# Window attention on one Trainium2 core: the order of exponentials, copies and a bias product inside a software pipeline

## The reference

```
xn = layernorm(h)
q, k, v = split(xn @ qkv_weight.T + qkv_bias)        # 64 windows, 8 heads, 128 x 8
attn = softmax(q * 8**-0.5 @ k.T + relative_bias)    # 64 x 8 matrices of 128 x 128
h = h + (attn @ v) @ proj_weight.T + proj_bias
```

## Time and profile before

| | us |
|---|---|
| median of 3 runs | 1490.92 (1488.49 to 1492.17) |
| the profiled execution's own time | 1492.72 |
| its span in the trace | 1490.8 |
| PE busy in the span | 1335.4 (90%) |
| DVE, ACT, POOL busy | 887.4, 860.3, 613.7 |

### The profile page before, as it was taken

One profiled execution on the slowest core, in us unless ns is written; L12 is line 12 of the kernel. 1 busy time (PEld: TensorE's weight loads), 2 busy tenths in 40 slices (PEclk: granted clock), 3 DMA queues, 4 the chain that ended last, 5 costly groups with the idle time before them and its releaser, 6 DMA issues.

```text
span 1490.8 us, 43422 instructions
## 1 busy us (share of the span) xinstructions
PE 1335.4 (90%) x15780; PEld 880.4 (59%) x15780; DVE 887.4 (60%) x2815; ACT 860.3 (58%) x2649; POOL 613.7 (41%) x967
## 2 busy tenths in 40 slices
PE   6998997888888888799999998799999999969998
PEld 2446874444444444577777777456666666446665
DVE  3775774555555555577878886234555555655664
ACT  3975663777777777455555555235555555635553
POOL 5000113555655655435555564412333333225554
PEclk9997996999999999899999999659999999969999
DMA  8300000000000000000000000000000000000001
GB/s 222 70 1 0 1 1 1 2 0 0 0 0 0 0 0 0 2 3 0 0 0 0 0 0 1 1 0 2 0 0 0 0 0 1 0 0 10 15 14 23
DMA packets 10094, 13.79 MB, mean 9 GB/s; under 512 B 9136, under 2 KB 9136, under 8 KB 9520
## 3 DMA queue, kind: packets, MB, share of 16 engines
q1 hardware_dynamic: 10032, 12.95, 3.5%
HBM read 10.85 MB, written 2.10 MB: 9 GB/s over the span
## 4 chain that ended last, share of the span: by engine, by line
PE 72%; ACT 10%; DVE 9%; issue 6%; POOL 1%; DMA 1%; ACTq 0%; DVEq 0%; POOLq 0%; SPq 0%
PE bank L1318 6%; PE bank L588 5%; PE bank L591 5%; PE bank L632 5%; PE bank L1655 4%; PE bank L145 4%; PE bank L1673 4%; PE bank L1312 4%; ACT big L689 3%; PE bank L1007 2%; PE bank L1277 2%; PE bank L1342 2%; ACT big L696 2%; PE bank L1034 2%; PE bank L324 2%
## 5 line engine op out<-in xcount | busy, mean ns | idle before, releaser
L527 POOL TENSOR_TENSOR big<-big 128x512 f32<-128x512 f32 x128 | 133.0, 1039 | 153.7 <-DVE big L725 153.6
L632 PE MATMUL bank<-cst,big 128*128 128x128 f32 x512 | 80.1, 279 | 53.5 <-ACT big L696 53.0
L632 PEld LDWEIGHTS bank<-cst,big 128*128 128x128 f32 x512 | 59.7, 142 | 104.5 <-issue 86.4
L1390 POOL TENSOR_TENSOR big<-g_a,g_b 64x64 f32 x128 | 40.0, 312 | 191.1 <-DVE g_a L1380 191.1
L929 POOL TENSOR_TENSOR big<-big 128x512 f32<-128x512 f32 x64 | 65.6, 1045 | 113.8 <-DVE big L1183 113.8
L689 ACT ACTIVATE big<-big 128x128 f32<-128x128 f32 x256 | 100.0, 405 | 1.2 <-DVE big L737 1.2
L1709 ACT ACTIVATE big<-bank 128x512 f32<-128x512 f32 x128 | 66.2, 603 | 50.4 <-PE bank L1655 50.4
L1576 POOL TENSOR_TENSOR big<-big 128x512 f32<-128x512 f32 x48 | 60.9, 1270 | 74.8 <-DVE big L1779 72.2
L1357 ACT ACTIVATE g_r<-bank,g_bias 128x64 f32<-128x64 f32 x128 | 40.2, 314 | 88.6 <-PE bank L1318 88.5
L689 ACT ACTIVATE big<-bank,big 128x128 f32<-128x128 f32 x256 | 90.5, 370 | 0.0
L1342 PE MATMUL bank<-cst 128*128 128x256 f32 (+1 forms) x256 | 88.3, 426 | 0.0
(11 more groups left out here) (271 smaller groups left out, 3661.1 us busy)
## 6 DMA issues: line engine op xcount, KB each, us to landing
big<-x_dram SPq DMA_DIRECT2D x12, 512.0 KB, 8.0
cst<-consts_dram SPq DMA_DIRECT2D x1, 3364.5 KB, 22.4
out_dram<-h SPq DMA_DIRECT2D x8, 256.0 KB, 2.6
cst<-consts_dram SPq DMA_DIRECT2D x3, 256.0 KB
cst<-consts_dram SPq DMA_DIRECT2D x1, 279.5 KB, 3.0
a_proj_padded<-consts_dram SPq DMA_DIRECT2D x8, 2.0 KB
cst<-consts_dram SPq DMA_DIRECT2D x8, 2.0 KB
cst<-consts_dram SPq DMA_DIRECT2D x2, 4.0 KB
```

Of the source, the lines that this page charges most:

```text
L527: nc.gpsimd.tensor_tensor(P, P, a_rs[t % 4].unsqueeze(2).to_broadcast([128, 4, 128]), ALU.mult).then_inc(a_n_r, 1)
L632: m = nc.tensor.transpose(bank(4)[:, 128 * k:128 * (k + 1)], a_P[tb % 4][:, 128 * k:128 * (k + 1)], eye)
```

## The change

Three reorderings, with no instruction added or removed. In PE, the bias product of an odd item t+1 leaves the odd slot t-1 (behind the scores) for the even slot t, behind the transposes and (if u is not 0) the attended product, and ahead of rows and projection. In ACT, the rows copy and the queries go behind the exponentials and the copy out of bank 4. In DVE, the copy out of bank 4 goes ahead of the keys and the addition to h.

```diff
@@ stage2_pe
             m = nc.tensor.matmul(scores_bank(t), a_q[l][r, :], a_kz[l][r, :], start=True, stop=not t % 2)
-            if t % 2:
-                m = nc.tensor.matmul(scores_bank(t), eye, c("a_bias", 512, 1024), start=False, stop=True)
-            m.then_inc(a_sc_r, 1)
+            if t % 2 == 0:
+                m.then_inc(a_sc_r, 1)
+
+        def bias(t):
+            nc.tensor.matmul(scores_bank(t), eye, c("a_bias", 512, 1024), start=False, stop=True).then_inc(a_sc_r, 1)
...
                 for d in (1, 2):
                     if exists(i, (t + d) // 8):
                         scores(i + (t + d) // 8, (t + d) % 8)
+            if t % 2 == 0 and exists(i, 0):
+                bias(t + 1)
             if u == 0:
@@ stage2_act
-            if u == 0 and exists(i, l, N2 - 1):
-                rows(i + l, 1 - l)
             ib, tb = back(i, t, 1)
...
                 m.then_inc(a_e_r, 1)
-            if u == 1 and exists(i, l, N2 - 1):
-                queries(i + l, 1 - l)
             ib, tb = back(i, t, 3)
             if tb % 2 and exists(ib, 0):
                 act.wait_ge(a_pt_r, ib * 8 + (tb + 1))
                 nc.scalar.copy(a_PT[tb % 4], bank(4)).then_inc(a_pta_r, 1)
+            if u == 0 and exists(i, l, N2 - 1):
+                rows(i + l, 1 - l)
+            if u == 1 and exists(i, l, N2 - 1):
+                queries(i + l, 1 - l)
@@ stage2_dve
+            ib, tb = back(i, t, 3)
+            if tb % 2 == 0 and exists(ib, 0):
+                v.wait_ge(a_pt_r, ib * 8 + (tb + 1))
+                if tb >= 4 or exists(ib, -1):
+                    v.wait_ge(a_av_r, ib * 8 + (tb - 3))
+                nc.vector.tensor_copy(a_PT[tb % 4], bank(4)).then_inc(a_ptd_r, 1)
             if u == 1 and exists(i, l, N2 - 1):
                 keys(i + l, 1 - l)
...
-            ib, tb = back(i, t, 3)
-            if tb % 2 == 0 and exists(ib, 0):
-                ...
-                nc.vector.tensor_copy(a_PT[tb % 4], bank(4)).then_inc(a_ptd_r, 1)
```

More of the change, by code:

```diff
@@ L746, in slot @@
                 nc.vector.tensor_tensor(hp, hp, bank(3)[:, 128:256].rearrange("p (b c) -> p b c", c=C), ALU.add).then_inc(a_h_r, 1)
-            ib, tb = back(i, t, 3)
-            if tb % 2 == 0 and exists(ib, 0):
-                v.wait_ge(a_pt_r, ib * 8 + (tb + 1))
-                if tb >= 4 or exists(ib, -1):
-                    v.wait_ge(a_av_r, ib * 8 + (tb - 3))
-                nc.vector.tensor_copy(a_PT[tb % 4], bank(4)).then_inc(a_ptd_r, 1)
             if isinstance(i, int) and i == N2 and t in (2, 4):
```

## The result

The changed kernel takes 1449.96 us (median of 4 runs, 1446.92 to 1451.30) against 1491.47 for the kernel before beside it: a ratio of 0.9727, 95% interval 0.9706 to 0.9748. Forecast were 1450 and a range of 1431 to 1468. Its profiled execution took 1446.92, with a span of 1445.0. The kernel was run again later, with 0.9701 (0.9682 to 0.9720).

A forecast was written before the change was run, and what follows sets the result against it. The prediction took a PE-ACT-PE loop, set by ACT's instruction order, as the bound. Halves fall from 11.21 to 9.9 us: 38 us, plus 3 in the first slots, makes 41, so 1450 us, range 1431 to 1468.

The forecast's parts named there:

- The loop through ACT's order: Stage 2, u = 0: ACT's copy out of bank 4 queued behind the rows copy; reordering regains 1.44 us per half.
- T0 - 0.5 to T0 + 0.8: When ACT was to start the exponentials after the change; T0 is the start of PE's transposes at u = 0.
- The bias product moved: PE's 0.96 us product goes to the even slot, moved but not saved; the 0.48 us wait at u = 3 goes.
- The wait on the spread: PE's scores at u = 3 wait for POOL's spread of the keys: new wait of 0.56 to 0.70 us per half.
- The sum: A half (four slots) takes 9.9 us, gaining 1.3; 29 halves give 38 us, first slots 3, total 41.
- The first slots: Start of the stage: a 1.98 us wait before the transposes goes, 2 us, plus 1 us from less idling.
- The drain stays as it is: The stage's end: no gain, since there are no rows to copy.
- The rule weighed: DVE's L251 with two SBUF inputs over a POOL product: no cost by the trace, about 6 us by the skill's rule.
- A: Rival: the spread's wait is hidden, a half takes 9.3 to 9.6 us, total 1433; chance 0.13.
- B: Rival: ACT is part of the loop again, a half takes 10.6 us, total 1471; chance 0.20.
- C: Rival: slower, PE waits at qkv for ACT's late rows copy; a half of 11.9 us gives 1511; chance 0.05.
- D: Rival: no change, something beside ACT's order such as POOL's queue sets the pace, 1491; chance 0.04.

The follow-up runs named there:

- experiment 1: The kernel before with only the ACT reordering (exponentials and copy out of bank 4 ahead of rows copy and queries): 1444.42 us, ratio 0.9710.
- experiment 5: The full change, but ACT's rows copy stands ahead of the exponentials again, queries still behind: 1493.95 us, ratio 1.0011 to the kernel before.
- experiment 4: The full change without DVE's part (its copy out of bank 4 behind the keys again): 1449.92 us, ratio 0.9729 to the kernel before.
- experiment 7: The full change, with POOL's spread waiting for a count four lower, the scores that last read its keys: 1428.22 us, ratio 0.9597 to the kernel before.
- act_relaxed: The kernel before with only ACT's reordering and the spread's wait count lowered by four: 1442.97 us, ratio 0.9681.
- two_inputs: The kernel before plus one DVE addition of two SBUF constants in slots with u = 3, beside POOL's products: 1488.34 us in one run.
- dve_only: The kernel before with only DVE's copy out of bank 4 moved ahead of keys and the addition to h: 1487.17 us, ratio 0.9989.
- experiment 9: The run two_inputs: the kernel before plus a DVE addition with two SBUF inputs beside POOL's products, 1488.34 us.

## Why the prediction was right

**The loop through ACT's order.** Right, and shown from both sides: ScalarE's part alone gives the gain (experiment 1), and putting one copy back takes it away (experiment 5). The prediction gave the whole 1.44 us at u = 1 to it; in the trace after, the transposes at u = 1 follow the attended product after 0.36 us, without a wait:
```profile
509.43 0.43 PE L607 MATMUL bank<-big 128*32 128x128 f32 x8
509.79 0.66 PE L634 MATMUL bank<-cst,big 128*128 128x128 f32 x4
```
ACT was even earlier than laid out: its exponentials started 0.94 us ahead of the transposes at u = 0 (516.31 against 517.25), where the text had T0 - 0.5 to T0 + 0.8:
```profile
516.31 0.38 ACT L691 ACTIVATE big<-bank,big 128x128 f32<-128x128 f32 x1
```
So the cover by the bias product in the slot with u = 0 was never needed, as experiment 1 shows without it.

**The bias product moved.** The prediction had 0.48 us back at u = 3 and 0.6 lost on the spread. By these two terms the move loses 0.12 us. Measured are 9.81 us for a half with the product left where it was (experiment 1) and 9.99 with it moved (experiment 4): a loss of 0.18 us, of which VectorE's part gives 0.06 back (9.93). The prediction did not draw the conclusion that this move was worth nothing, though its own terms said so, and it gave VectorE's part no term of its own.

**The wait on the spread.** Foreseen at 0.56 to 0.70 us, taken as 0.6. The idle rows of PE give 0.50, and 0.1 more goes in the longer pair of scores (1.23 in place of 1.13). Experiment 7 takes exactly this wait away and gets 0.66 us of each half back. That it came from the place of the bias product follows from `act_relaxed`: with the product in its old place the looser count changes nothing in a half.

**The sum.** 9.9 us for a half was forecast and 9.93 measured; 29 x 1.3 = 38 against 36.0 in 28 halves and some 1.3 in the last. The first slots gave 5.0 in place of 3, as the clock no longer fell to 1.2 GHz there (granted 1.00 from 250 to 260 us after, 0.50 from 255 to 260 before); the text had 0 to 3 us for that and took 1, and it was the upper end. The drain gave 2 us in place of 0. "The drain stays as it is" was wrong for its slots: the wait of 0.4 us at u = 3 stood there too (595.06 to 595.90 before) and is gone, and PE needs 0.6 us less up to its first product of stage 3 with fX (L999 at 601.02, L1003 at 558.15). The other 1.3 us lie behind that product, where PE runs with long waits. Busy time from it to the mark behind the drain, before and after (columns as in the earlier trace rows):
```profile
601.02:618.57 17.55, 11.34 (x74) 7.89 (x71) 9.85 (x14) 3.40 (x7) 6.58 (x10) 0.65 0.00 1
558.15:574.37 16.22, 9.54 (x73) 5.99 (x70) 9.85 (x14) 3.53 (x7) 6.79 (x11) 0.79 0.00 1
```
DVE does the same work, PE takes 1.8 us more for its own at a granted clock of 0.65 against 0.79. Why the clock was lower there is not shown; the traces of `two_inputs` and `dve_only`, with PE's and ACT's order of before, had 38.5 and 38.4 us from the last L566 on in place of 39.2.

So the sum was right where the change acts, and that the median came out at 1449.96 for a forecast of 1450 is in part luck. Between the two traces lie 45.8 us and not 41: 2 more in the first slots, 2 in the drain, 1.6 behind it, 0.7 less in the halves. The 41.5 us between the two medians are less, because the profiled execution of before was 1.3 us above the median of its kernel, and that of the change 3.0 below. One bound of the forecast's own range was also summed wrongly: a wait of 0.3 us and 5 us in the first slots give 1450 - 29 x 0.3 - 2 = 1439, not 1442. The range of 1431 to 1468 does not hang on it.

**The rule weighed.** It had been given 6 us if L251 came to lie over a GpSimd product. It did not: L251 stayed at 424 to 426 ns, and L527 at 1035 to 1042, as DVE's reciprocal, for which GpSimd waits, comes right behind L251. In both traces each of the 14 L251 ends 0.2 us before the next L527 starts (before: 282.33 + 0.42 against 282.92). The rule itself holds (experiment 9). What the rows of before showed was that the two never met, not that meeting is free: the sentence "by the row the overlap costs nothing" was wrong.

**The rivals.** A (spread hidden, 1433) would have been seen as halves under 9.6; B and C as waits of L632 on L696 or of L572 on the rows copy. None of them is in the trace. D would have left the halves at 11.2.

## What to carry to other kernels

When one engine idles before an instruction that needs the newest result, and work that needs only old results stands behind it in the same queue, swap the two; here a copy of 0.27 us in the wrong place cost 3% of the program. Look up what a moved instruction counts for: the bias product raised a semaphore on which a third engine waited, four items stricter than needed, and that wait, not the product's own 0.96 us, decided whether the move paid. Test the parts of a reordering one by one: two of three here were worth nothing by themselves, and the bias move paid only after a wait outside the change was loosened. Whether VectorE's part is needed then was not run. And where the whole time moves by 2 us and more between traces for other reasons, judge such a change by the stretch in which it acts.

## What the runs showed that I had not expected

The chain of waits is of no help once a software pipeline is full: in the trace after, between 500 and 512 us, it leads through GpSimd and "issue", although PE was 95% busy from 400 to 500, and 100% with the spread's wait loosened (experiment 7), so that nothing else of GpSimd held it up. Its head in that window (pieces that reach over the edge count whole, so the shares add up to more than 100%):
```profile
by line: issue 65.9%; POOL big L527 35.2%; POOL rstd L269 5.8%; POOL h L509 3.4%; POOL big L513 3.0%; POOL eps_var L267 1.8%; POOLq L525 1.2%; POOL big L521 1.1%; POOLq L513 0.5%; POOLq L512 0.3%; POOLq L266 0.3%; POOLq L268 0.3%; POOLq L26
```
There the distances between the starts of one line, once per half, told more: in the three kernels that ran twice a half came out the same to 0.01 us (9.93, 9.81, 9.27), where medians of whole runs moved by 4 us (ScalarE's part: 1444.42 and 1449.01, with ratios of 0.9710 and 0.9709).
